# Expert layers with finished rows routed block by block into per-expert DRAM regions, and W1 by DMA per block

## What is computed

```python
def _unipool_layer(xt, router, W1, W2):          # W1 (16,128,512), W2 (16,512,128)
    logits = xt @ router
    probs = softmax(logits)
    w, idx = max(probs), argmax(probs)
    for i in range(16):
        out += where(idx == i, w, 0)[:, None] * (silu(xt @ W1[i]) @ W2[i])
    return out
xt = _layernorm(x)
for router in routers: xt = _unipool_layer(xt, router, W1, W2)
x = x + xt
```

## Time and profile before

| | |
|---|---|
| median of three runs | 573.17 us (569.8 to 573.19) |
| span of the profiled execution | 577.5 us |
| busy: PE, PEld | 490.8 us, 400.5 us |
| busy: DVE, ACT, POOL | 330.0 us, 276.8 us, 196.7 us |
| DMA moved | 28.12 MB, mean 49 GB/s |
| longest shares of the chain that ended last | PE L806 18%, PE L793 18%, PE L635 6% |

### The profile page before, as it was taken

The page is one execution under the profiler, slowest core; times in us unless marked ns, Lnnn a source line. Parts: engine busy times, 40 slices in busy tenths (PEclk is TensorE's granted clock), DMA queues, the critical chain, the costliest instruction groups (busy, mean ns, idle before and its releaser), DMA issues.

```text
span 577.5 us, 16903 instructions
## 1 busy us (share of the span) xinstructions
PE 490.8 (85%) x5788; PEld 400.5 (69%) x5788; DVE 330.0 (57%) x746; ACT 276.8 (48%) x684; POOL 196.7 (34%) x243
## 2 busy tenths in 40 slices
PE   1589999999787769999868999976899986799894
PEld 1367877787554338999435999733899953589892
DVE  2468777877658684455185455339345526645452
ACT  1277766777672316665103666410566610266550
POOL 8222332231030154235325405503532541541352
PEclk9999999999999889999997999978899999799998
DMA  5542223300000201001301100120110130100005
GB/s 142 178 130 85 66 86 94 93 5 4 3 1 2 73 18 35 24 20 40 91 1 37 33 8 37 41 74 5 42 31 10 39 100 3 32 28 16 24 37 159
DMA packets 37315, 28.12 MB, mean 49 GB/s; under 512 B 5105, under 2 KB 33137, under 8 KB 37233
## 3 DMA queue, kind: packets, MB, share of 16 engines
q1 hardware_dynamic: 33136, 18.62, 11.2%
q0 software_dynamic: 4096, 8.40, 4.6%
HBM read 20.71 MB, written 6.29 MB: 47 GB/s over the span
## 4 chain that ended last, share of the span: by engine, by line
PE 59%; DVE 15%; issue 7%; DMA 6%; ACT 5%; POOL 3%; another core or an unknown queue 2%; SPq 1%; DVEq 0%; POOLq 0%; ACTq 0%
PE bank L806 18%; PE bank L793 18%; PE bank L635 6%; PE bank L616 4%; DMA cur<-token_rows 3%; PE bank L594 3%; DVE ohr L1083 2%; DVE ppT L910 2%; DMA ppT<-token_rows,token_i 2%; DMA token_rows<-ysort,token_i 2%; PE bank L588 1%; PE bank L575 1%; PE bank L564 1%; PE bank L782 1%
## 5 line engine op out<-in xcount | busy, mean ns | idle before, releaser
L1132 DVE SCALAR_TENSOR_TENSOR pp<-pp,bank 128x512 f32<-128x512 f32 x124 | 85.3, 688 | 126.8 <-ACT pp L531 116.0
L806 PE MATMUL bank<-w,pp 128*128 x992 | 136.3, 281 | 9.0 <-DVE pp L1132 6.9
L793 PE MATMUL bank<-vm,ppT 128*128 x992 | 137.4, 283 | 0.0
L806 PEld LDWEIGHTS bank<-w,pp 128*128 128x128 f32 x992 | 122.5, 194 | 11.7 <-issue 10.9
L793 PEld LDWEIGHTS bank<-vm,ppT 128*128 128x128 f32 x992 | 125.1, 198 | 1.6 <-issue 0.5
L531 ACT ACTIVATE pp<-bank 128x512 f32<-128x512 f32 x124 | 74.1, 598 | 95.6 <-PE bank L793 77.8
L522 ACT COPY ppT<-w 128x512 f32 x124 | 75.8, 611 | 60.2 <-DVE piece_tile L1105 59.7
L389 POOL DMA_INDIRECT token_rows<-ysort,token_i x64 | 62.1, 971 | 102.9 <-DVE ysort L1142 85.2
L382 POOL DMA_INDIRECT ppT<-token_rows,token_i x64 | 61.7, 964 | 64.2 <-PE bank L782 41.3
L689 PE MATMUL bank<-trib,onesb 128*128 128x512 bf16 x308 | 77.4, 409 | 0.0
L446 ACT ACTIVATE pp<-bank,nmax 128x128 f32<-128x128 f32 x256 | 68.0, 426 | 0.0
(11 more groups left out here) (182 smaller groups left out, 522.8 us busy)
## 6 DMA issues: line engine op xcount, KB each, us to landing
w<-in_L_ffn_W_dram SPq DMA_DIRECT2D x32, 256.0 KB, 3.4
cur<-token_rows SPq DMA_DIRECT2D x16, 256.0 KB, 3.6
cx<-in_ctx_dram SPq DMA_DIRECT2D x16, 128.0 KB, 2.4
token_rows<-cur SPq DMA_DIRECT2D x1, 1024.0 KB, 5.0
ppT<-token_rows,token_i POOLq DMA_INDIRECT x64
token_rows<-ysort,token_i POOLq DMA_INDIRECT x64
out_dram<-xs SPq DMA_DIRECT2D x4, 256.0 KB, 2.7
xs<-in_x_dram SPq DMA_DIRECT2D x1, 768.0 KB, 6.1
```

Of the source, the lines that this page charges most:

```text
L793: last = mm(banks[2 + j % 2][:, c * P:(c + 1) * P], w1_piece[:, j % 2, c * P:(c + 1) * P], xT[:, ds(tile_of[j] * P, P)], start=True, stop= ...
L806: last = mm(banks[6 + j % 2][:, 0:D], hh[:, j % 2, c * P:(c + 1) * P], w2[:, ds(e * FF + c * P, P)], start=(c == 0), stop=(c == FC - 1))
L1132: v.scalar_tensor_tensor(hh[:, j % 2, :], th[:, j % 2, :], 1.0, banks[2 + j % 2][:, :], ALU.add, ALU.mult).then_inc(s["h_ready"], 1)
```

## The change

The 31 pieces of a layer become 31 blocks. A block is up to 128 rows of one expert. For each expert there is a region of DRAM (17 regions of 2,176 rows, two copies for alternate layers). A row in DRAM now has 274 floats (1,096 B): 128 features, 16 logits for the next layer, a stamp, the token's number and the 128 features of the residual. As soon as a block's output is there, PE transposes it and multiplies with the next layer's router; every four blocks (a part; three and one at the end) DVE chooses experts and computes places, with PE's rank products, and POOL scatters the rows into the regions of the next layer. DVE makes the block table after the last part; SP waits for all scatters, then loads each block's rows and each block's W1 (by DMA out of the input array, four buffers). Rows past an expert's end come from a padded part, have a large stamp, and are thrown out by the scatter's bounds check. Silu is taken in one ACT instruction; the probability comes from the carried logits by a tanh in four groups of blocks a layer. The last layer scatters block by block into the output. The hardware loop is gone: the four layers are written out.

```diff
-        w1 = sb("w1", [P, E * FF])
-        xs = sb("xs", [P, NT, D])
-        cur = sb("cur", [P, NT, D])
+        slots = sb("slots", [P, BLOCKS, ROW])
+        w1_staged = sb("w1_staged", [P, 4, FF])
+        parts = [list(range(a, min(a + 4, 24))) for a in range(0, 24, 4)] + [[24, 25, 26], [27, 28, 29], [30]]
+        gate_groups = [(0, 4), (4, 10), (10, 20), (20, BLOCKS)]
+        gate_steps = [0, 4, 9, 16]
...
         @block.sync
-                    sp.dma_start(w1[:, e * FF:(e + 1) * FF], W1[e]).then_inc(s["w1_loaded"], 16)
+            for region in regions:
+                sp.dma_start(region.rearrange("(e r) c -> r e c", r=REGION)[0:P, :, :],
+                             slots[:, BLOCKS - 1, :].unsqueeze(1).broadcast_to([P, E + 1, ROW])) \
+                    .then_inc(s["pads_written"], 16)
+            def load_rows(layer, j):
+                row = entry(block_row, j, mybir.EngineType.SP, E * REGION)
+                sp.dma_start(slots[:, j, :], regions[layer % 2][ds(row, P), :]).then_inc(loaded[j], 16)
+            def load_weights(layer, j):
+                n = layer * BLOCKS + j
+                e = entry(block_expert, j, mybir.EngineType.SP, E - 1)
+                if n >= 4:
+                    sp.wait_ge(s["h_mm"], n - 3)
+                sp.dma_start(w1_staged[:, n % 4, :], W1[ds(e, 1), :, :].rearrange("a d f -> (a d) f")) \
+                    .then_inc(w1_here[n % 4], 16)
+            for layer in range(L):
+                sp.wait_ge(s["scattered"], 16 * (NT + layer * BLOCKS))
+                sp.wait_ge(s["tables_ready"], 2 * layer + 2)
+                for j in range(4):
+                    load_weights(layer, j)
+                    load_rows(layer, j)
+                for j in range(4, BLOCKS):
+                    load_rows(layer, j)
+                for j in range(4, BLOCKS):
+                    load_weights(layer, j)
...
         @block.gpsimd
+            def scatter_part(number, of_part, region):
+                wait_alone(pool, s["place_ready"], number + 1)
+                for j in of_part:
+                    g.indirect_dma_start(
+                        out=region, out_offset=bass.IndirectOffsetOnAxis(ap=place_i[:, j:j + 1], axis=0),
+                        in_=slots[:, j, :], in_offset=None, bounds_check=E * REGION - 1, oob_is_err=False) \
+                        .then_inc(s["scattered"], 16)
...
         @block.scalar
+            def silu(layer, j):
+                n = layer * BLOCKS + j
+                act.wait_ge(s["h_mm"], n + 1)
+                if n >= 2:
+                    act.wait_ge(s["y_mm"], n - 1)
+                a.activation(hh[:, n % 2, :], banks[2 + n % 2][:, :], ACT.Silu).then_inc(s["h_ready"], 1)
...
         @block.tensor
+            def hidden(layer, j):
+                n = layer * BLOCKS + j
+                pe.wait_ge(s["xT_evac"], n + 1)
+                pe.wait_ge(w1_here[n % 4], 16 * (n // 4 + 1))
+                if n >= 2:
+                    pe.wait_ge(s["h_ready"], n - 1)
+                for c in range(FC):
+                    last = mm(banks[2 + n % 2][:, c * P:(c + 1) * P], w1_staged[:, n % 4, c * P:(c + 1) * P],
+                              xTs[:, n % 2, :], start=True, stop=True)
+                last.then_inc(s["h_mm"], 1)
+            for layer in range(L):
+                expert_of = {}
+                pe.wait_ge(s["tables_ready"], 2 * layer + 2)
+                for i in range(BLOCKS + 4):
+                    if i < BLOCKS:
+                        expert_of[i] = entry(block_expert, i, mybir.EngineType.PE, E - 1)
+                        turn(layer, i)
+                    if 0 <= i - 1 < BLOCKS:
+                        hidden(layer, i - 1)
+                    if layer < L - 1 and 0 <= i - 3 < BLOCKS:
+                        turn_output(layer, i - 3)
+                    if layer < L - 1 and 0 <= i - 4 < BLOCKS:
+                        next_logits(layer, i - 4)
+                    if 0 <= i - 2 < BLOCKS:
+                        output(layer, i - 2, expert_of.pop(i - 2))
...
+                                ranks(part_number(layer, m), len(of_part))
+                if layer < L - 1:
+                    stay_warm(banks[7], 30)
...
         @block.vector
+                for i in range(BLOCKS + 6):
+                    if i < BLOCKS:
+                        evac_xT(layer, i)
+                    if i in gate_steps:
+                        gate_shift(layer, gate_steps.index(i))
+                    if i - 1 in gate_steps:
+                        gate_finish(layer, gate_steps.index(i - 1))
...
+                    if layer < L - 1 and 0 <= i - 4 < BLOCKS:
+                        evac_logits(layer, i - 4)
+                    if 0 <= i - 2 < BLOCKS:
+                        evac_y(layer, i - 2)
+                    if layer < L - 1:
+                        for m, of_part in enumerate(parts):
+                            if of_part[-1] == i - 5:
+                                put(part_number(layer, m), of_part, False)
+                        for m, of_part in enumerate(parts):
+                            if of_part[-1] == i - 4:
+                                choose(part_number(layer, m), of_part)
+                if layer < L - 1:
+                    make_tables()
```

More of the change, by code:

```diff
@@ L267, in _ @@
+            sp.wait_ge(s["stored"], 16 * BLOCKS)
         @block.gpsimd
@@ L536, in _ @@
-            layers(act, one_layer)
+            for q in (0, 2):
+                act.wait_ge(s["t_done"], 4 + q + 1)
+                a.copy(curT[:, q * 512:(q + 1) * 512], banks[q][:, :]).then_inc(s["t_evac"], 1)
+            a.preload_act_table(ACT.Silu)
+            def silu(layer, j):
[4 more added lines that the diff above has]
+                a.activation(hh[:, n % 2, :], banks[2 + n % 2][:, :], ACT.Silu).then_inc(s["h_ready"], 1)
@@ new lines, in output, with turn_output @@
+            def output(layer, j, e):
+                n = layer * BLOCKS + j
+                pe.wait_ge(s["h_ready"], n + 1)
+                if n >= 1:
+                    pe.wait_ge(s["y_evac"], n)
+                for c in range(FC):
+                    last = mm(banks[5][:, 0:D], hh[:, n % 2, c * P:(c + 1) * P],
+                              w2[:, ds(e * FF + c * P, P)], start=(c == 0), stop=(c == FC - 1))
+                last.then_inc(s["y_mm"], 1)
+            def turn_output(layer, j):
+                n = layer * BLOCKS + j
+                pe.wait_ge(s["y_evac"], n + 1)
+                if n >= 1:
+                    pe.wait_ge(s["yT_evac"], n)
+                nc.tensor.transpose(banks[4][:, 0:P], tile_n(j), ident[:]).then_inc(s["yT_mm"], 1)
```

595 lines of the change are left out of this document (260 added, 335 removed).

## The result

The changed kernel takes 658.96 us (median of 4 runs, 656.45 to 660.53), the kernel before 571.48 us in the same comparison (4 runs, 568.91 to 573.19). The ratio is 1.153, with a 95% interval of 1.147 to 1.160: slower by 15%. The prediction was 644 us, between 577 and 705, and slower with a chance of 0.85. The profiled execution of the changed kernel has a span of 658.8 us.

The account below looks back on a forecast made before the run. SP's in-order list, with 35 issues ahead of weight 4, stalls TensorE in every layer; otherwise PE bounds. 219 + 335.7 (layers 0 to 2) + 89.9 (layer 3) + 3.4 = 648, less 4.3: 644 us, range 577 to 705.

Parts of the forecast that it names:

- The pair on SP: SP's list at each layer's start: register read plus issue, 0.85 us each, 35 of them ahead of weight 4.
- rival (b): SP's list: row loads issue much faster, so weight 4 isn't late and no stall comes; 559 us, chance 0.10.
- rival (a): SP's list: the read is hidden and a pair costs 0.47 us, or transfers bind alike; 590 us, chance 0.18.
- Rival (c): SP's list: a pair is dearer, 1.12 us with the longest read; 682 us, up to 705, chance 0.15.
- The stall: Each layer's fifth hidden product waits for weight 4 until 33.4 us after SP may load, against 14.2 unstalled.
- the start of a layer: Unstalled, from SP's first load to the fifth product: 4.9 us to the first product and four blocks of 2.33.
- The pace: PE's products after the stall: 2.33 us a block in layers 0 to 2, 1.90 in the last, PE the bound.
- the 5.2: Products' stretch of each layer: 5.2 us for filling the pipeline and a half-clock start, expected after the stall.
- The gap: Between layers, from the last W2 product to SP's loads: 10.4 us of output, routing, scatters and landing.
- The start of layer 0: Routing and sixteen scatters after the attention and scan stages: SP loads from 219 us.
- the pads take about 17 us, hidden: Two pad writes, 4.8 MB, beside a stage with DMA share 0.24: hidden, 17 us if they were not.
- From span to median: End of the sum: the earlier runs' median lay 4.3 us below the profiled execution, so 4.3 comes off 648.

Follow-up runs that it names:

- Experiment 4: Changed kernel, but SP reads the row number once for rows 4 to 30: row loads every 0.47 us in place of 0.81, layer 0's hole 4.5 us; no time given.
- experiment 3: Changed kernel, but loads of rows 4 to 30 in layers 1 to 3 fetch 584 of 1,096 bytes a row: 659.0 us in one run.
- experiment 1: Changed kernel with only SP's order changed: weight 4 behind eight rows in place of 31, then two rows and a weight by turns: 592.48 us.
- experiment 2: Changed kernel with weight 4 behind 17 rows in place of 31, then two rows and a weight by turns: 611.0 us in one run.
- experiment 6: Against experiment 1: weights 0 to 3 asked for ahead of the wait for the scatters, first four gates after the second turned-block copy: 580.3 us.
- experiment 7: Against experiment 1: gates worked out four blocks at a time, in place of groups of 4, 6, 10 and 11: 582.8 us.
- experiment 10: Changed kernel with weights asked for by ScalarE, 0 to 3 once the block table is there; SP keeps rows in their old order: 575.9 us.

## Why the prediction was right, step by step

**The pair on SP: right.** 0.85 us was chosen between 0.75 and 0.98; it is 0.81, and 0.83 on average with the slower ones among the 35. The read is 0.27, as bare as on ACT and DVE, and the issue 0.33, shorter than the 0.47 of the earlier trace rows, with 0.2 between them. Experiment 4 shows that read and issue add up. One reading in front of it was wrong: 0.47 was not the shortest issue. The trace of the kernel before has fixed issues of 0.37 and 0.43 us on SP, close to the 0.41 at which rival (b) would have begun. What kept (b) out is the read on top of each issue.

**The read and the issue in two other prices.** The reads on SP have a median of 0.275 and 0.273 us. The Trainium skill (DMA: Bandwidth & Descriptors, Latency and other measured facts) gives a floor of about 0.6 us for a `tensor_load`, which made 689 us; the measurement decides against it here. A row load moves 137 KB in some 0.5 us by the earlier trace rows and occupies SP for 0.81, and experiment 3 shows that the issue binds. The Trainium skill (the same page, Issuing engines are not separate DMA queues) says that a sequencer's issue time is usually small beside the DMA, which stood beside rival (a), 590; it is not small in this list. Rival (c), a dearer pair, falls with the reads.

**The stall: right.** The fifth product was put at 33.4 us after the first issue; it is 31.8 to 32.3. The 35 pairs took 28.9 to 29.5 us in place of 29.8, and from weight 4's issue to the product it was 2.7 to 2.9 in place of 3.7. What the stall is worth was overrated: 19.2 us a layer and 2 of half clock by the prediction, from an unstalled start of 14.2 us. With the order mended alone the start took 17.9, and a layer gained 16.6 us (66.5 / 4). For the same reason the hole is 13.3 to 14.4 us and not the 15 to 25 that were named as its sign. Rival (b), which assumed that the hole is not there, would by experiment 1 have come out near 592 and not at 559: slower than before even so. The step that failed there is the start of a layer: 4.9 us to the first product and 2.33 a block left out that the second product waits for row 3 through the gates on DVE (2.2 us) and that the first products run at half clock. That is 3.7 us a layer, some 15 of the 33; the others are layer 0's start, the last layer and the step from span to median, below.

**The pace: right, the sum behind it in part by luck.** 2.33 was predicted as the average with rank products. A step takes 2.23 us and one with rank products, mostly every fourth, 2.42, so about 2.28; the last layer has 1.90 exactly. From the fifth product to the last W2 product's end layer 0 takes 68.4 us, by the prediction 62.9 + 5.2 = 68.1. But the 5.2 were to be filling and half clock, and these took 1.9 and 1.7. Two waits for the gates on DVE, which the prediction had at nothing, took 3.3 more, and the shorter step gave 1.3 back over 27 steps. DVE does not become the bound, but the gates hold PE up in bursts (10.9 us in all in layers 0 to 2). ScalarE's table swaps, put at nothing with up to 10 us kept in the range, did not come: no table is loaded after 199.4 us.

**The gap: right.** 10.4 predicted, 10.8 measured, by the same chain: last product, routing, POOL's scatters one behind the other, landing, SP.

**The periods** are 110.9, 111.9 and 112.4 us against 111.9 each. The last layer with the end took 95.5 against 93.3: chiefly three waits for the gates (0.95, 1.07 and 0.64 us) and 2.8 us in place of 1.5 for the last scatter to land, less 1.5 from the earlier fifth product.

**The start of layer 0: wrong by 9.1 us.** 219 was predicted, 228.1 measured. Scatters and routing account for 2: the first scatter came 5.6 us after curT and not 4.6, and SP's first issue 22.6 after it and not 21.6. The other 7.1 are there before the last residual (166.40 in place of 159.27): 4.7 between tiles 9 and 11, which the pads cost, 1.7 of half clock at the last tile, and 0.7 that was late from the first tiles on. The step that failed is "the pads take about 17 us, hidden": the transfers did take about 17 us (113 to 131 us) and stood beside other work, but that work grew longer by 4.4 to 4.7 us. A share of 0.24 over the whole stage did not show that the engines would be full for 16 us (share 0.99, 310 GB/s from 114 to 130 us). Part of the 9.1 is this execution: in the seven other profiles with the same code and pads up to there (experiments 1 to 4, 6, 7 and 10) the first scatter came at 200.0 to 203.2 us, here at 205.5; predicted was 197.4.

**From span to median.** The prediction took 4.3 us off because the profiled execution of before lay above its median. That belonged to that execution; the changed kernel's span of 658.8 is that of the slowest of its four, and its median is 658.96. So 644 missed by 15: 9.1 from layer 0's start, 2.2 from the last layer, 4.3 from this, less 0.5 in the periods.

## What to carry to other kernels

Count the issues ahead of each load in its queue, in the order in which they stand, and multiply by the whole cost of an issue with its register read (here 0.81 us): a prefetch of everything that is cheap can bar the one load that is needed next, and the whole pipeline stands behind it. Interleave such lists at the pace at which they are consumed, or put them on two engines; here the same transfers in another order gave back 66 of 87 us. When a hole is mended, cost the start that lies under it: waits that it covered (first gates, half clock, late weights) come up next; here these, with the pads moved and smaller last groups, were worth another 38 us.

## What the runs showed of the hardware that was not expected

- An issue with an address out of a register took 0.33 us on SP and 0.34 on ACT, less than the 0.37 to 0.47 of most fixed ones in the attention stage; back to back without a read, issues took 0.38 and were 0.47 apart (experiment 4).
- A row load's time to land was longer with more in flight (medians): 2.3 us at one per 0.81 us, 3.3 at one per 0.47 (experiment 4), and 3.6 at one per 0.81 with weights between them from ScalarE (experiment 10).
- Large writes in the background stopped TensorE without a visible releaser, 1.0 us of delay for 2.4 MB and 4.4 for 4.8 MB. Packets of an instruction queue came 8.6 to 9.5 us apart in place of 5.8 meanwhile, and each stop ended 1.3 to 1.6 us after one had landed.
- An indirect scatter of 128 rows of 1,096 B took POOL 0.97 us, and 1.28 from one to the next: as long as the indirect DMAs of the kernel before, and in layer 0 sixteen of them in a row are 20 us on the path.
